# Adding each tile's rows straight into the output by an accumulating scatter, in place of put rows and a later sum

## The reference

```python
scores = softmax(mask @ G)                       # 8 experts
value, indices = top_k(scores, 2)                # 2 experts for each token
gated = silu(mask @ gate_w[e]) * (mask @ up_w[e])
out_e = gated @ down_w[e].T + (mask @ lora_A[e].T) @ lora_B[e].T
return x + sum over the two chosen e of value[e] * out_e
```

## Time and profile before

| | |
|---|---|
| time, median of 3 runs (lowest to highest) | 814.0 us (810.34 to 814.15) |
| profiled execution: span | 807.6 us |
| busy: PE, DVE, ACT, POOL | 65%, 64%, 56%, 48% |
| mean DMA rate over the span | 198 GB/s |
| chain of waits, largest shares | DMA 25%, POOL 18%, issue 15%, DVE 14%, PE 13% |

### The profile page before, as it was taken

One profiled execution on the slowest core, in us unless ns is written; L12 is line 12 of the kernel. 1 busy time (PEld: TensorE's weight loads), 2 busy tenths in 40 slices (PEclk: granted clock), 3 DMA queues, 4 the chain that ended last, 5 costly groups with the idle time before them and its releaser, 6 DMA issues.

```text
span 807.6 us, 14610 instructions
## 1 busy us (share of the span) xinstructions
PE 521.7 (65%) x4178; PEld 356.3 (44%) x4178; DVE 515.2 (64%) x1242; ACT 453.9 (56%) x655; POOL 390.2 (48%) x337
## 2 busy tenths in 40 slices
PE   0311287179878872787889817887888278888900
PEld 0300276066545542555546515554556155555500
DVE  5768889757597675765786776657773623232345
ACT  5687387749844574387445654883456145455500
POOL 8114200115375222577887125878872168768510
PEclk9855599579999995899999958997999779999965
DMA  9990160024323553478478834685579249858469
GB/s 313 359 265 0 58 256 27 13 65 157 111 78 126 200 223 121 131 246 288 155 246 265 351 113 145 230 292 173 192 259 372 79 147 311 270 189 279 179 252 382
DMA packets 80443, 159.93 MB, mean 198 GB/s; under 512 B 22889, under 2 KB 32105, under 8 KB 79856
## 3 DMA queue, kind: packets, MB, share of 16 engines
q1 hardware_dynamic: 59760, 108.60, 39.0%
q0 software_dynamic: 20608, 50.37, 17.9%
HBM read 107.53 MB, written 73.40 MB: 224 GB/s over the span
## 4 chain that ended last, share of the span: by engine, by line
DMA 25%; POOL 18%; issue 15%; DVE 14%; PE 13%; ACT 7%; DVEq 3%; SPq 3%; POOLq 1%; ACTq 0%
DMA out_dram<-piece 7%; DMA piece<-put_rows 7%; DMA put_rows<-y,where 5%; POOL piece L528 4%; POOL piece L531 4%; ACT mask L793 3%; PE pa L678 3%; DMA xg<-mask_rows,where 3%; POOL xg L511 3%; POOL put_rows L519 2%; DVE w L1169 2%; DMA w<-put_rows 2%; DVE mask L1063 2%; ACT y L850 2%; PE pb L665 2%
## 5 line engine op out<-in xcount | busy, mean ns | idle before, releaser
L678 PE MATMUL pa<-w,xt 128*128 x1472 | 198.7, 289 | 1.9 <-issue 1.8
L678 PEld LDWEIGHTS pa<-w,xt 128*128 128x128 f16 x1472 | 146.8, 100 | 58.2 <-issue 12.9
L850 ACT ACTIVATE y<-pc,where 128x512 f32<-128x512 f32 x184 | 124.1, 686 | 78.9 <-PE pc L704 58.7
L511 POOL DMA_INDIRECT xg<-mask_rows,where x92 | 98.8, 1074 | 125.6 <-DVEq L1331 95.2
L519 POOL DMA_INDIRECT put_rows<-y,where x92 | 92.5, 1005 | 134.1 <-ACT y L850 112.6
L1339 DVE SCALAR_TENSOR_TENSOR g_full<-pa,where,s_act 128x144 f32<-128x144 f32 x92 | 33.6, 365 | 185.2 <-ACT s_act L842 184.8
L837 ACT ACTIVATE xt<-pb 128x1024 f16<-128x1024 f16 x92 | 94.2, 1024 | 99.0 <-PE pb L665 96.3
L665 PE MATMUL pb<-ident,xg 128*128 128x128 f16 x736 | 62.1, 233 | 68.7 <-DMA xg<-mask_rows,where 47.8
L665 PEld LDWEIGHTS pb<-ident,xg 128*128 128x128 f16 x736 | 49.2, 105 | 79.7 <-DMA xg<-mask_rows,where 53.3
L842 ACT ACTIVATE s_act<-pa,small 128x128 f32<-128x128 f32 x92 | 33.8, 368 | 87.1 <-PE pa L678 87.1
L701 PE MATMUL pc<-wd,gt 128*128 x184 | 76.0, 413 | 5.1 <-ACT y L850 4.6
(11 more groups left out here) (208 smaller groups left out, 879.2 us busy)
## 6 DMA issues: line engine op xcount, KB each, us to landing
piece<-put_rows SPq DMA_DIRECT2D x96, 256.0 KB, 3.9
v<-in_x_dram SPq DMA_DIRECT2D x40, 512.0 KB, 9.0
piece<-in_x_dram SPq DMA_DIRECT2D x48, 256.0 KB, 2.9
out_dram<-piece SPq DMA_DIRECT2D x48, 256.0 KB
mask_rows<-mask SPq DMA_DIRECT2D x4, 2048.0 KB, 17.2
w<-put_rows SPq DMA_DIRECT2D x16, 512.0 KB, 9.5
w<-in_L_ffn_gate_w_dram SPq DMA_DIRECT2D x8, 512.0 KB, 10.2
w<-in_L_ffn_up_w_dram SPq DMA_DIRECT2D x8, 512.0 KB, 8.3
```

The source lines that it names most:

```text
L511: pool.indirect_dma_start(out=xg[:, g % NX, :], out_offset=None, in_=mask_rows[n % 2], in_offset=bass.IndirectOffsetOnAxis(ap=mask_row[n][ ...
L678: last = pe.matmul(l1[g % 2], xt[:, g % 2, t, :], w1[:, bass.ds(e, 1), t, k, :].rearrange("p o n -> p (o n)"), start=(t == 0 and k == 0), ...
L850: nc.scalar.activation(y[:, g % NY, half * HALF:(half + 1) * HALF], pc[:, half, :], ACT.Copy, scale=y_scale[n][:, i:i + 1]).then_inc(y_rea ...
```

## The change

Four `fill_out(n)` DMAs copy each batch of `x` to `out`, HBM to HBM. Each tile then has one indirect DMA that adds its rows of `y` into `out` (`add_out`, `compute_op=ALU.add`). As two tiles can hold the same output row, each add waits on GpSimd until the add before it has landed, over all 92 tiles. `put_rows`, `piece`, `sum_piece`, the loads and stores of pieces and the sum of the last batch are gone. `y` has 5 buffers. An idle slot now has a valid row: it gathers the mask row of its own slot number, its scale is zero, and it adds zeros to a row of another batch (of batch 1 in stage 0, else of batch 0). So every gather and every add is of 128 rows.

```diff
-    NX, NY = 3, 2
-    PIECES, NC = 2 * C, 2
+    NX, NY = 3, 5
+    PUTS = 1
+    PUT_COLS = H // PUTS
...
-        piece = sb("piece", [P, NC, 3, HALF], F32)
-        spare = piece[:, :, :, :].rearrange("p i k h -> p (i k h)")
+        spare = y[:, 0:3, :].rearrange("p i h -> p (i h)")
-        parts_B = y[:, :, :].rearrange("p i h -> p (i h)").bitcast(F16)
+        parts_B = y[:, 3:5, :].rearrange("p i h -> p (i h)").bitcast(F16)
...
+            def fill_out(n):
+                sp.dma_start(out[n], x[n]).then_inc(out_filled[n], 16)
...  (in move_mask: the last load of x is gone; then the order on SP)
+            fill_out(0)
             for n in range(B):
+                move_mask(n)
+                if n + 1 < B:
+                    fill_out(n + 1)
+                    sp.wait_ge(scores_ready, n + 1)
+                    load_t(n + 1)
+            for n in range(B):
+                sp.wait_ge(out_filled[n], 16)
+            for k in range(PUTS):
+                sp.wait_ge(added[k], 16 * T * B)
...
+            def add_out(n, i):
                 g = tile(n, i)
+                for k in range(PUTS):
+                    pool.wait_ge(y_ready, 2 * g + (k + 1) * 2 // PUTS)
+                    if g > 0:
+                        pool.wait_ge(added[k], 16 * g)
+                    pool.indirect_dma_start(
+                        out=all_out,
+                        out_offset=bass.IndirectOffsetOnAxis(ap=put_row[n][:, i:i + 1], axis=0),
+                        in_=y[:, g % NY, k * PUT_COLS:(k + 1) * PUT_COLS], in_offset=None,
+                        element_offset=k * PUT_COLS, bounds_check=B * S - 1, oob_is_err=True,
+                        compute_op=ALU.add).then_inc(added[k], 16)
...
-                if n >= 2:
-                    pool.wait_ge(summed_piece, PIECES * (n - 1))
+                pool.wait_ge(out_filled[n], 16)
+                if n == 0:
+                    pool.wait_ge(out_filled[1], 16)
                 for i in range(T):
...
                     if i >= 3:
-                        put_out(n, i - 3)
+                        add_out(n, i - 3)
...
-                    if n > 0 and i in PIECE_AT:
-                        sum_piece(n - 1, PIECE_AT[i])
...  (store_y)
-                if g >= NY and half == 0:
-                    act.wait_ge(put[g % NY], 16 * (g // NY))
+                if g >= NY and half % (2 // PUTS) == 0:
+                    act.wait_ge(added[half * PUTS // 2], 16 * (g - NY + 1))
...  (take_slots)
-                V.tensor_scalar(none_here, pair, 0.0, SKIP, ALU.is_equal, ALU.mult)
-                V.tensor_scalar(second_here, pair, float(S), -float(S), ALU.is_gt, ALU.mult)
+                own, idle = float(n * S), float(S if n == 0 else 0)
+                V.tensor_scalar(none_here, pair, 0.0, row_1, ALU.is_equal, ALU.mult)
+                V.tensor_scalar(idle_here, pair, 0.0, idle - own, ALU.is_equal, ALU.mult)
...
-                V.tensor_copy(put_row[n], none_here)
-                V.tensor_tensor(mask_row[n], none_here, second_here, ALU.add)
+                V.tensor_copy(mask_row[n], none_here)
+                V.scalar_tensor_tensor(put_row[n], idle_here, own, none_here, ALU.add, ALU.add)
...  (the 16 additions of the last batch on DVE are gone)
```

More of the change, by code:

```diff
@@ L28 @@
 EXPONENT = 0x7F800000
-SKIP = 4096.0
 AIM = 28.0
@@ L99, in build @@
     MAX_AT = {(19, 2): 0, (20, 0): 1, (20, 1): 2, (20, 2): 3, (21, 0): 4, (21, 2): 5, (22, 0): 6, (22, 2): 7}
-    PIECE_AT = {**{j + 1: j for j in range(9)}, **{j + 4: j for j in range(9, PIECES)}}
-    PIECES_FIRST = 14
     with ExitStack() as ctx:
@@ L201, in build @@
         tiles_below, tiles_to = temp(E), temp(E)
-        none_here, second_here = temp(T), temp(T)
+        none_here, idle_here = temp(T), temp(T)
         tile_past = temp(T * E).rearrange("p (j e) -> p j e", j=T)
@@ L211, in cell @@
             return small[:, cells[0] - n:cells[0]]
-        expert_no, tile_no, token_1 = cell(E), cell(T), cell(C)
+        expert_no, tile_no, token_1, row_1 = cell(E), cell(T), cell(C), cell()
         lower = cell(E * E).rearrange("p (a e) -> p a e", a=E)
@@ L267, in build @@
         mask_rows = [nc.dram_tensor(f"mask_rows{i}", [S, H], F16, kind="Internal").ap() for i in range(2)]
-        put_rows = [nc.dram_tensor(f"put_rows{i}", [ROLES * S, H], F32, kind="Internal").ap() for i in range(2)]
         x_landed = [sem(f"x_landed{c}") for c in range(C)]
@@ L294, in build @@
         gathered = [sem(f"gathered{i}") for i in range(NX)]
[L295 to L301, removed]
+        out_filled = [sem(f"out_filled{n}") for n in range(B)]
+        added = [sem(f"added{k}") for k in range(PUTS)]
         xt_turned, xt_ready, l1_done, silu_done = (
@@ L307, in build @@
         x_rows = x.rearrange("b (p c) h -> b p c h", c=C)
[L308 to L312, removed]
+        all_out = out.rearrange("b s h -> (b s) h")
         side_rows = side.rearrange("b (p c) o -> b p (c o)", c=C)
@@ L381, in move_mask @@
                     load_x(n + 1)
-                else:
-                    for c in range(C):
-                        sp.dma_start(v[:, c, :], x_rows[n][:, c, :]).then_inc(last_x_landed[c], 16)
                 if n >= 2:
@@ L389, in move_mask @@
                              mask[:, :]).then_inc(mask_stored, 16)
-            move_mask(0)
-            sp.wait_ge(scores_ready, 1)
-            load_t(1)
+            fill_out(0)
             for n in range(B):
[L396 to L426, removed]
+                move_mask(n)
[7 more added lines that the diff above has]
+                sp.wait_ge(added[k], 16 * T * B)
         @block.gpsimd
@@ L439, in _ @@
             nc.gpsimd.iota(token_1.bitcast(I32), pattern=[[1, C]], base=1, channel_multiplier=C)
+            nc.gpsimd.iota(row_1.bitcast(I32), pattern=[[0, 1]], base=1, channel_multiplier=1)
             nc.gpsimd.iota(slot_int.bitcast(I32), pattern=[[1, P]], base=0, channel_multiplier=0)
@@ L447, in _ @@
                                     base=0, pattern=[[1, P]], channel_multiplier=-1)
-            for ints in (expert_no, tile_no, token_1):
+            for ints in (expert_no, tile_no, token_1, row_1):
                 nc.gpsimd.tensor_copy(ints, ints.bitcast(I32))
@@ L514, in gather @@
                     bounds_check=S - 1, oob_is_err=False).then_inc(gathered[g % NX], 16)
-            def put_out(n, i):
+            def add_out(n, i):
                 g = tile(n, i)
[L518 to L532, removed]
+                for k in range(PUTS):
[8 more added lines that the diff above has]
+                        compute_op=ALU.add).then_inc(added[k], 16)
             for n in range(B):
@@ L551, in _ @@
                             below_third(n + 1, q)
-                    if n > 0 and i in PIECE_AT:
-                        sum_piece(n - 1, PIECE_AT[i])
                 for i in range(T - 3, T):
-                    put_out(n, i)
+                    add_out(n, i)
         @block.tensor
@@ L1265, in weigh @@
                         dve.drain()
-                for r in range(ROLES):
-                    V.tensor_scalar(vals[:, :, r, 0], token_1, float(r * S), None, ALU.add)
+                V.tensor_copy(vals[:, :, :, 0], token_1.unsqueeze(2).to_broadcast([P, C, ROLES]))
                 V.tensor_copy(vals[:, :, :, 4], power.unsqueeze(2).to_broadcast([P, C, ROLES]))
@@ L1438, in _ @@
                     route(n + 1)
[L1441 to L1448, removed]
 _INS = ['x', 'fside_BxSx1_0', 'cond_2048', 'L0_ffn_G', 'L0_ffn_gate_w', 'L0_ffn_up_w',
```

## The result

The changed kernel takes 960.3 us (median of 4 runs, 958.5 to 962.8), the one before 814.1 beside it: 1.179 times as long, 95% interval 1.173 to 1.186. The direction was forecast, the size wasn't: 845 us, with a range up to 935. Each run's time stands 1.7 to 1.8 us above its own span (958.2 us of span are 959.95).

A forecast was written before the change was run, and what follows sets the result against it. No engine filled a stage; tiles took 4.9 to 5.7 us. Chained adds at 6.1 us each, with 14, 14 and 3 us of lag, handovers and a 6 us end, gave 839.2 us of span, plus 6.4: 845 us, range 780 to 935.

The forecast's parts named there:

- the release: On GpSimd, from one add's landing to the next add's issue: 0.76 us.
- L: Time of one add from issue to landing, with the next gather hidden inside: 5.3 us, bounded by 4.1 and 6.6.
- routing hidden by the late chain: At stage handovers, the next stage's first gather follows the last add by 1.3 us, not 13.
- the short end: After the last put, 35.8 us shrink to one landing and about 0.7 us, together 6.0 us.
- the sum: Whole kernel's span, added up from first put, four stages, handovers and end: 839.2 us.
- the high end: Upper bound for an add: a full read with its own issue wholly ahead of the put, 6.6 us to landing.
- The rival that stood on it: Each add's second read costs its data and nothing else: 4.7 us to landing, 796 us in all; chance 0.24.
- P: Period of the chain of adds, landing time plus release on GpSimd: 6.1 us a tile.
- a lag of 14, 14, 3 and 0: Delay in us of the adds in stages 0 to 3 by x, mask and fill moving beside the chain.
- The rival "read and put in series": Each add's read comes wholly before its put: 6.6 us to landing, period 7.4, 961 us; chance 0.12.
- break-even: Point where the change neither gains nor loses: an add landing in 4.98 us, a period of 5.74.
- What goes: GpSimd's 96 additions of pieces and most of the 35.8 us end: about 60 us, if adds were free.

The follow-up runs named there:

- run 1: Changed kernel with the addition dropped from its scatters, which write plainly in the same chain of waits; 775.5 us, 0.947 times the kernel before.
- run 5: Changed kernel with each add one iteration later in GpSimd's order, so gathers are issued one add earlier; 962.0 us against 960.3.
- run 2: Changed kernel with half the bytes per add, in two edits: half the columns, 851.7 us, and half the rows, 828.1 us.
- run 8: Kernel before with unchained puts; batches 0 to 2 summed by accumulating DMAs from put rows to out, which no tile awaits; 795.7 us, 0.976 times before.
- run 9: Kernel before with the additions of batch 2's pieces moved from GpSimd to DVE in stage 3; 817.2 us, 1.004 times before.

## Why the prediction was right in kind and wrong in size

- **The mechanism held.** A chain of landings, the release on top, gathers inside L, routing hidden by the late chain, the short end: each is in the trace, and run 1 (no addition), run 5 (no effect of the order) and run 2 (shorter landings, a shorter period) leave no other for the bulk of the 146 us. The bottom line was slower, as forecast, with a chance of 0.62.
- **The step that failed is the term L,** "rounded with the issue overlap to L = 5.3". It is 6.2. The other terms of the sum were nearly right: fixed 1.1 beside the issue, and the half adds of 4.9 and 4.7 against 6.2, each less its issue, give 1.3 to 1.4 us for half the data, so 2.7 where I had 2 x 1.3. 6.2 - 1.6 - 1.1 - 2.7 leaves 0.8 us, where I had 0.7 for a read from HBM; that it is this read is not shown. What was missing is 0.6 us of issue (1.59 against 1.0): I took a put's issue for an add's. I had named the issue only in the high end. And 5.4 was rounded down for an overlap that isn't there: by the packets in the traces, a lone add's data start 2.16 us after the start of its issue and a put's 1.58, so the longer issue comes on top.
- **The Trainium skill's rule** (Collectives: The Full Stack, "The bandwidth ceiling: the fold count and why AG ≠ RS ≠ AR"), a reduce reads twice and the add itself is free, agrees for the data part: 2.7 us for an add, 1.3 for a put. The rival that stood on it (L = 4.7, 796 us) left out the 0.6 us of issue and the 0.8 us that remain, and was wrong.
- **The release** was 0.88 us, put at 0.76. P is 7.05 against 6.1. Over 88 intervals this is 84 of the 119 us by which the span (958.2) misses the sum (839.2). Alone it would have made 930 us, just inside the range; what follows took the time out of it.
- **The moves beside the chain** are the second miss. Above 22 x 7.05 the intervals of the stages are 23.5, 23.8, 6.2 and 4.8 us longer, 58 in all, where I had a lag of 14, 14, 3 and 0. Of the 58 the two slow adds of each of the first two stages and one of stage 2 make 43, 12 more than I had. I counted a fill as 4 MB at 388 GB/s, 11 us. The fill of batch 0, issued at 59 us in the quiet stretch, took 15.5 us, and the changed kernel's fills 30.1 in the median.
- **GpSimd's other work** was put at nothing: "and so do `diagonal` and `below_third`". The release is 0.84 to 0.88 us in most adds, but a few start later, 8 us later in all. 5 of these are behind `below_third` (2.5 us from landing to issue in the rows of 236.99 to 245.71). The last 8 of the 58 us are single landings somewhat over 6.2.
- **The rest:** handovers of 30.4, 30.7 and 23.1 us from last to first add, 4 us over; an end of 9.4 us, 3.4 over, of which some 3 us come after the last landing and stay unexplained; 0.4 at the start. 84 + 27 (12 + 8 + 8, rounded) + 4 + 3.4 + 0.4 = 119. Of the 6.4 us that I added to the span only 1.8 belong to every run; the profiled execution before was a quick one.
- **The rival "read and put in series" gave 961 us, and it is a coincidence.** It needed L = 6.6 and P = 7.4; with the measured P of 7.05 the same sum gives 930. Too long an L made up for the short lag and for GpSimd's work.
- **My break-even was too kind.** It stood at L = 4.98, P = 5.74. The half-column run has L = 4.9 and, with a release of 0.88, P = 5.8, and takes 851.7 us. Its stages take 69 us more than 88 x 5.75, where I had 31: the moves and `below_third` delay a shorter chain too.
- **What goes:** the end was right, 28 us less in run 1. The 29 us that I gave to the pieces in stages 1 to 3 can't be read from it, as its chain binds too. In run 8, without pieces, the put intervals of these stages are 122.5, 120.9 and 97.9 us, where they were 123.2, 124.7 and 106.9: 13 us. A gain that stands in the sum and not under what goes is the routing hidden by a chain: 30 us in run 1.

## What to carry to other kernels

Before a step is made to wait for a DMA's landing, multiply landing and release by the number of steps, and compare with the time that a step takes now: here 7.05 us against 4.9 to 5.7. Additions in DMAs that no step waits for can be longer each and yet faster in all (run 8). What else runs on the issuing engine, and what moves beside the chain, comes on top of each period that it meets. An experiment that moves work to an engine in the step's own path tests that path too (run 9). For an operation without a row, take its issue apart from its data and put a bound on each, and keep the sum of the terms as it comes out.

## What the runs showed of the hardware

- An indirect accumulating DMA of 128 rows costs GpSimd 1.59 us of issue, of 64 rows 1.45, a plain one 1.0; a direct accumulating DMA of 512 KB costs 0.99.
- From issue to landing, an indirect add of 512 KB from SBUF to HBM takes 6.2 us; with half the bytes 4.7 to 4.9; with no row 2.7; the plain write of 512 KB 3.3.
- An add of 128 slots, of which idle ones are skipped by an index out of bounds, landed in 6.2 us with 0.21 MB, like a full one.
- Two adds of half columns in flight land in 5.0 us each, issued 2.4 us apart; one alone lands in 4.9.
- An add that meets 4 MB of x, 2 MB of mask and 4 MB of HBM-to-HBM fill landed in 22.1 us; without the fill in 11.8. A plain write in that stretch landed in 21.8. Of the puts before, with no fill beside them, none took over 10.2.
